# Second biases of a mixture-of-experts block: fp32 products over 8 rows, or fp32r products over 16 rows

## The reference, cut to what matters

```python
combine = jnp.sum(jax.nn.one_hot(idx, E) * w[..., None], axis=-2)          # (tokens, 8)
p1 = jnp.einsum('bsh,eoh->bseo', nf, mlp1_weight) + mlp1_bias
...
act = g * jax.nn.sigmoid(ALPHA * g) * (lin + 1.0)
p2 = jnp.einsum('bsei,ehi->bseh', act, mlp2_weight) + mlp2_bias            # second bias: (8, 256)
combined = jnp.einsum('bseh,bse->bsh', p2, combine)
```

## Time and profile before

| what | value |
|---|---|
| time, median of 3 runs | 1203.12 us (1199.26 to 1204.91) |
| the profiled execution's own time | 1205.98 us |
| its span | 1204.1 us |
| TensorE matmuls busy | 974.9 us (81%) |
| VectorE busy | 828.1 us (69%) |
| ScalarE busy | 697.5 us (58%) |
| GpSimd busy | 424.8 us (35%) |
| mean clock granted to TensorE, share of full | 0.906 |

### The profile page before, as it was taken

The page is one execution under the profiler, slowest core; times in us unless marked ns, Lnnn a source line. Parts: engine busy times, 40 slices in busy tenths (PEclk is TensorE's granted clock), DMA queues, the critical chain, the costliest instruction groups (busy, mean ns, idle before and its releaser), DMA issues.

```text
span 1204.1 us, 18696 instructions
## 1 busy us (share of the span) xinstructions
PE 974.9 (81%) x5241; PEld 414.1 (34%) x5313; DVE 828.1 (69%) x1622; ACT 697.5 (58%) x905; POOL 424.8 (35%) x360
## 2 busy tenths in 40 slices
PE   4608897889679897987778997888799999996564
PEld 1302222233233443333233343323343344344243
DVE  5732102669658797677676799586867897797797
ACT  2318895856448574765448665675567676771232
POOL 2413303433244333533235333542232333233243
PEclk9858998989889999988799898999989899997587
DMA  4254454324424252434413345352534353421011
GB/s 150 74 108 79 102 104 99 88 74 97 116 59 130 77 117 82 102 96 95 119 37 103 98 108 118 71 128 67 114 86 107 97 125 82 101 76 58 31 53 31
DMA packets 80001, 110.08 MB, mean 91 GB/s; under 512 B 22523, under 2 KB 56707, under 8 KB 76803
## 3 DMA queue, kind: packets, MB, share of 16 engines
q1 hardware_dynamic: 61444, 83.47, 29.9%
q10 hardware_dynamic: 18432, 25.17, 7.0%
HBM read 82.89 MB, written 25.69 MB: 90 GB/s over the span
## 4 chain that ended last, share of the span: by engine, by line
PE 49%; DVE 25%; issue 13%; ACT 4%; DMA 3%; POOL 2%; SPq 2%; another core or an unknown queue 1%; DVEq 0%; ACTq 0%; POOLq 0%
PE OP L687 13%; PE S L673 12%; PE D L659 8%; DVE th_sb L1103 3%; DVE act_sb L1108 3%; PE A L642 3%; PE D L569 3%; PE D L586 3%; PE BB L642 3%; DVE acc L1098 2%; DVE g_sb L1086 2%; DVE l_sb L1088 2%; DMA X<-in_x 2%; DVE xn L946 2%; ACT probs L804 2%
## 5 line engine op out<-in xcount | busy, mean ns | idle before, releaser
L804 ACT ACTIVATE probs<-S 128x1024 f32<-128x1024 f32 x512 | 511.8, 1022 | 256.2 <-PE S L673 253.4
L673 PE MATMUL S<-Qs,Ks 98*128 98x512 bf16 x1024 | 312.4, 399 | 61.8 <-issue 23.0
L687 PE MATMUL OP<-probs,V 128*17 128x512 f32 x2048 | 280.1, 620 | 2.7 <-ACT O L813 2.7
L891 POOL TENSOR_TENSOR act_lo<-act_sb,act_hi 128x512 fp32r<-128x512 f32 x128 | 165.5, 1293 | 212.3 <-DVE act_hi L1114 152.4
L673 PEld LDWEIGHTS S<-Qs,Ks 98*128 98x128 bf16 x1024 | 81.4, 101 | 249.0 <-ACT probs L804 98.7
L659 PE MATMUL D<-W,act_hi 128*128 128x256 f32 x448 | 135.6, 333 | 29.5 <-DVE Vn L986 16.2
L1098 DVE SCALAR_TENSOR_TENSOR acc<-D,combh,acc 128x256 f32<-128x256 f32 x224 | 97.1, 475 | 82.5 <-PE D L659 82.1
L1103 DVE SCALAR_TENSOR_TENSOR th_sb<-th_sb,g_sb 128x512 f32<-128x512 f32 x128 | 129.6, 1012 | 0.7 <-ACT th_sb L780 0.7
L885 POOL TENSOR_SCALAR W<-W2b 128x512 fp32r<-128x512 bf16 x64 | 45.4, 709 | 217.4 <-PE D L659 212.1
L1108 DVE SCALAR_TENSOR_TENSOR act_sb<-l_sb,th_sb 128x512 f32<-128x512 f32 x128 | 107.2, 837 | 16.7 <-POOL act_lo L891 12.2
L659 PE MATMUL D<-W,act_lo 128*128 128x256 f32 x448 | 116.3, 290 | 0.0
(11 more groups left out here) (136 smaller groups left out, 1016.7 us busy)
## 6 DMA issues: line engine op xcount, KB each, us to landing
W<-in_w ACTq DMA_DIRECT2D x64, 256.0 KB, 2.7
Ks<-k_scr SPq DMA_DIRECT2D x32, 384.0 KB
W2b<-in_w ACTq DMA_DIRECT2D x64, 128.0 KB, 2.7
Ks<-k_scr SPq DMA_DIRECT2D x32, 256.0 KB
o_scr<-O SPq DMA_DIRECT2D x32, 256.0 KB, 4.5
q_scr<-parts SPq DMA_DIRECT2D x16, 384.0 KB, 3.1
k_scr<-parts SPq DMA_DIRECT2D x16, 384.0 KB, 2.6
Qs<-q_scr SPq DMA_DIRECT2D x32, 192.0 KB
```

The source lines that it names most:

```text
L673: last = mm(S[:, j2, C * i:C * (i + 1)], Ks[0:SROWS + MROWS, g % 2, j, P * kt:P * (kt + 1)], Qs[0:SROWS + MROWS, g % 2, j, :], start=True, ...
L687: last = mm(OP[32 * j:32 * j + VW, :], V[:, kt, HG * g + j, :], probs[:, s % 2, C * j:C * (j + 1)], start=kt == 0, stop=kt == KT - 1)
L804: nc.scalar.activation(probs[:, s % 2, 2 * C * j2:2 * C * (j2 + 1)], S[:, j2, :], ACT.Exp, scale=SCALE).then_inc(exp_done, 1)
L891: tt(act_lo[:, e % 2, it, :], act_sb[:, a % 2, :], act_hi[:, e % 2, it, :].bitcast(FP32), ALU.subtract).then_inc(lo_s, 1)
```

## The change

The combine weights are split into two fp32r parts that together carry the fp32 value, and lie side by side as 16 columns; the bias table is loaded twice, into rows 0 to 7 and 8 to 15, and made fp32r. One product over 16 rows then gives the sum of both parts. The transposes treat the 16 columns as fp32. In `gates2` the sum of the two masks now goes back to `oh1`; a copy rounds it to the first part, `combh` is computed from `oh1`, and a subtraction makes the second part. One more small load is issued near the start.

```diff
-        b2_sb = sb("b2_sb", [NE, E], BF16)
-        b2f = sb("b2f", [NE, E], FP32)
+        b2_sb = sb("b2_sb", [2 * NE, E], BF16)
+        b2f = sb("b2f", [2 * NE, E], FP32R)
...
-        combT = sb("combT", [NE, C], FP32)
+        combT = sb("combT", [2 * NE, C], FP32R)
...
+        comb = sb("comb", [P, TC, 2, NE], FP32R)
...
-        N_LOADS, N_LATE = 6, 11
+        N_LOADS, N_LATE = 6, 12
...
-                (b1_sb[:, :, :, :], b1), (b2_sb[:, :], b2), (rank[:, :], ...
+                (b1_sb[:, :, :, :], b1), (b2_sb[0:NE, :], b2), (b2_sb[NE:2 * NE, :], b2), (rank[:, :], ...
...
-                    pe.wait_ge(comb_s, 3 * (u + 1))
+                    pe.wait_ge(comb_s, 4 * (u + 1))
                     for t in range(TC):
-                        last = nc.tensor.transpose(bank[0:NE, P * t:P * (t + 1)], comb[:, t, :], ident[:, :])
+                        last = nc.tensor.transpose(bank[0:2 * NE, P * t:P * (t + 1)],
+                                                   comb[:, t, :, :].rearrange("p a e -> p (a e)").bitcast(FP32), ident[:, :])
...
-                    v.tensor_copy(combT[:, :], bank[0:NE, :]).then_inc(combT_s, 1)
+                    v.tensor_copy(combT[:, :], bank[0:2 * NE, :]).then_inc(combT_s, 1)
...
-                v.tensor_tensor(comb[:, :, :], oh1[:, :, :], oh2[:, :, :], ALU.add).then_inc(comb_s, 1)
-                dve.wait_ge(comb_s, 3 * u + 1)
-
-                v.tensor_scalar(combh[:, :, :], comb[:, :, :], 0.5, None, ALU.mult).then_inc(comb_s, 2)
+                v.tensor_tensor(oh1[:, :, :], oh1[:, :, :], oh2[:, :, :], ALU.add).then_inc(comb_s, 1)
+                dve.wait_ge(comb_s, 4 * u + 1)
+                v.tensor_copy(comb[:, :, 0, :], oh1[:, :, :]).then_inc(comb_s, 1)
+                v.tensor_scalar(combh[:, :, :], oh1[:, :, :], 0.5, None, ALU.mult).then_inc(comb_s, 1)
+                dve.wait_ge(comb_s, 4 * u + 3)
+                v.tensor_tensor(comb[:, :, 1, :], oh1[:, :, :], comb[:, :, 0, :].bitcast(FP32), ALU.subtract).then_inc(comb_s, 1)
```

More of the change, by code:

```diff
@@ L274, in block_kernel @@
         lgb = sb("lgb", [P, TC, NE], BF16)
-        lgt, pick, oh1, oh2, lg2, comb, combh = (
-            sb(n, [P, TC, NE], FP32) for n in ("lgt", "pick", "oh1", "oh2", "lg2", "comb", "combh"))
+        lgt, pick, oh1, oh2, lg2, combh = (
+            sb(n, [P, TC, NE], FP32) for n in ("lgt", "pick", "oh1", "oh2", "lg2", "combh"))
+        comb = sb("comb", [P, TC, 2, NE], FP32R)
         S = ps("S", [P, 2, 2 * C], FP32)
@@ L403, in _ @@
                 (gate_b_sb[:, :], gate_b[None, :].to_broadcast([P, NE])),
-                (b1_sb[:, :, :, :], b1), (b2_sb[:, :], b2), (rank[:, :], rank_in[None, :].to_broadcast([P, NE])),
+                (b1_sb[:, :, :, :], b1), (b2_sb[0:NE, :], b2), (b2_sb[NE:2 * NE, :], b2), (rank[:, :], rank_in[None, :].to_broadcast([P, NE])),
                 (Ks[SROWS:SROWS + MROWS, :, :, :].rearrange("p s j t -> p (s j t)"), ones_in),
```

## The result

The changed kernel takes 1192.89 us (median of 7 runs, 1189.29 to 1194.83), the kernel before 1203.12 in the same session: a ratio of 0.992, 95% interval 0.9895 to 0.9945, so 0.8% faster and clear of the 0.5% that can be told apart. The profiled execution took 1192.6 us, with a span of 1190.8 and a mean granted clock of 0.918 (0.906 before). The forecast was 1198.0 with a range of 1191 to 1205: the time lies in the range and the direction was right, but the likeliest case, no measurable change, did not come; by the medians the gain is twice the 5.1 us that I summed.

The account below looks back on a forecast made before the run. No single engine was taken to bound the kernel: the chain passes between TensorE (49%) and VectorE (25%). Stages -5.2, additions +1.8 and tail -1.7 us sum to -5.1, from 1203.12 to 1198.0 us, range 1191 to 1205.

Parts of the forecast that it names:

- Where the change lies: Chain holds gates2 and the second b2 stage in chunks 1 to 5, that stage in 6 and 7, both stages in the tail.
- What a stage costs: On TensorE, a b2 stage in fp32r takes 0.43 us at full clock, 0.59 at half; 1.06 and 2.00 before.
- What of it reaches the chain: Second b2 stages of seven chunks: 4.2 to 6.2 us won, 5.2 taken, with ScalarE's exponentials limiting some chunks.
- The additions: Extra VectorE operations in gates2: 0.31 to 0.40 us more in each of the first five chunks, 1.8 us lost in all.
- The tail: Chunk 8, both b2 stages on the chain: 0.9 to 2.45 us won after the added VectorE work, 1.7 taken.
- The sum: Whole kernel: -5.2 + 1.8 - 1.7 = -5.1 us, giving 1198.0 us from the median of 1203.12.
- The clock: Rival: two long slow TensorE stretches of 6.8 us each don't come, 6.8 us more won, 1191 us; chance 0.19.
- The slower rival: TensorE, idler around the second stage, loses its clock more often: even at 1203 us (chance 0.13) or slower, 1209.9 (0.08).
- The gain hidden behind ScalarE: Rival: ScalarE holds TensorE's start behind the stage, so chunks give at most about 2 us, 1202 us; chance 0.08.

Follow-up runs that it names:

- e3: Changed kernel with the first b2 stage of each chunk back in fp32 over 16 rows, only the second in fp32r: 1193.61 us, 0.9934 of the kernel before.
- e4: Changed kernel with the second b2 stage of each chunk back in fp32 over 16 rows, only the first in fp32r: 1200.82 us, 0.999 of the kernel before.
- e5: Changed kernel with fp32r products in the last chunk alone, fp32 over 16 rows in the other seven: 1202.08 us, 0.9972 of the kernel before.
- e9: Changed kernel with the transposes and first b2 stage one half-step earlier (31 and 32), the second left at 34: 1198.4 us, 0.9963 of the kernel before.
- fp32 twin: Kernel before, fp32 over 8 rows without the split, with transposes at 31, first stage at 32, second at 34: 1199.67 us, 0.9972 of the kernel before.
- e7: Changed kernel with all products in fp32 over 16 rows and those of the second b2 stage made twice: 1214.55 us, 1.0089 of the kernel before.
- e1: Changed kernel with all second-bias products back in fp32 over 16 rows, only the additions left: 1202.32 us, 1.0001 of the kernel before.
- e2: Changed kernel with only the rounded first part of the combine weights in 8 rows, no copy, subtraction or second load: 1192.53 us, 0.9913 of the kernel before.
- e10: Changed kernel with four more dependent 128 x 32 VectorE operations in gates2: 1205.08 us, 1.0007 of the kernel before.
- e8: Changed kernel with the second b2 stage one half-step later (35 in place of 34): 1208.24 us, 1.0033 of the kernel before.

## Why the prediction was right and wrong

**Where the change lies: right.** The second stage is on the chain in all seven chunks, the first in the tail alone; e3, e4 and e5 show it, and e9 with its fp32 twin shows that the gain goes when the place is covered.

**What a stage costs: right at full clock.** 0.43 us, as read from the experts' products; 16 rows cost the same as 8 and as 128. At half clock I had 0.59 and the rows show 0.70 to 0.73.

**What of it reaches the chain: a mis-sized term.** I had 4.2 to 6.2 us and took 5.2. The seven stages lost 6.6 us from start to scores. Two things were off. I had capped the chunks 1 and 2 at 0.65 and 0.44 us by ScalarE's exponentials; in the changed kernel's first chunk the scores start at 246.83, while the exponential runs from 246.55 to 247.55, so those scores don't wait for it and the cap was a misreading. And the middle between the two prices was a compromise: the rows of the traces, of e7 too, point to the price at the clock of the place.

**The additions: the other mis-sized term.** I had 0.31 to 0.40 us in five chunks, 1.8 in all, and nothing in 6 and 7. Up to the copy of combT the rows show 0.19 to 0.25 us in every chunk, so the links were cheaper than I had read (0.22, not 0.31, behind a wait). But at the second stage only 0.12 us is left in chunk 1, 0.05 to 0.07 in 2 to 5 and nothing in 6 and 7: 0.4 us. I had taken gates2 as on the chain link by link and not asked what slack lies behind it, between the copy of combT and the copy to acc. Why VectorE is faster there in chunks 1 to 5 is open; the rows show that it is. In chunk 7 the transposes stood 2.1 us, not 3, behind the last of the operations in the kernel before (1034.34 after 1032.27); nothing came of it.

**The tail: a little low.** 1.39 + 1.42 was expected at half clock and (1.98 - 0.70) + (2.01 - 0.73) = 2.6 us measured, 2.3 with the additions, against the 1.7 taken.

**The sum.** 6.6 - 0.4 + 2.3 = 8.5 us, where I had summed 5.1: both main terms erred to the same side. The medians differ by 10.2 us and the ratio says 9.6, with 6.6 to 12.6 as its interval. Taken from the rows directly, as the time from the router's result to the scores behind the second stage, over the seven chunks and the tail, this is what each kernel differs by from the kernel before, beside what its ratio gives:

| kernel | rows, us | ratio, us |
|---|---|---|
| changed | -8.5 | -9.6 |
| e1, all products fp32 | -0.6 | +0.1 |
| e2, one part | -9.4 | -10.5 |
| e3, second stage fast | -7.4 | -7.9 |
| e4, first stage fast | +0.2 | -1.2 |
| e5, tail fast | -2.2 | -3.4 |
| e7, second stage doubled | +10.5 | +10.7 |
| e10, four more operations | -0.5 | +0.8 |

The rows come from one execution of each kernel, all against the same one of the kernel before, and carry about 1 us of chance, the ratios 2 to 3 us; no kernel is off by more than 1.4. So the time of this stretch accounts for the results as well as they are known.

**The clock: the rival that may have taken part.** I gave 0.19 to the clock being lost less often, as a case of its own that ends at 1191, and the measured 1192.89 is nearer to that than to the forecast. I had also named as a sign of being wrong a mean clock that differs from 0.906 by more than 0.005. In the profiled execution it is 0.918, so this sign came. Between the two profiled executions, whose times differ by 13.4 us, the slow stretches differ by 13.7 us, just the two long ones of the rival. Over all runs the mean clock rose less, from 0.910 to 0.915. Over 214 runs of all kernels here, taken within each kernel, a run whose mean clock is 0.001 higher is 0.47 us shorter; 0.005 makes 2.3 us. Added to the 8.5 of the rows, which hold a part of it already, that is 10.8, and with or without it the sum lies in the interval of 6.6 to 12.6. For e10 it makes 9.3 us out of 7.4, where 10.5 was measured. This is a relation between runs, not an experiment: no run here changed the clock and nothing else. But runs of both kernels with the same clock can be compared: at 0.911 and 0.912 the three of the changed kernel have a mean of 1193.7 us and the twelve of the kernel before 1201.8, so 8.1 us of gain are there without any more clock. So the direct part is shown; the clock's share is argued, and why the clock moved is open.

**The slower rival: did not come.** TensorE did become idler in front of the second stage (2.32 us after 1.85), as I had said, and the clock was not lost more often. For this rival I had read that the clock falls behind the long idle times and not behind the short one. Chunk 6 of the kernel before speaks against it: the wait is as short as in chunk 7, and the clock is at half for 6.8 us all the same.

```profile
932.92 1.37 PE L612 MATMUL D<-b2f,combT 8*128 8x256 f32 x4 [0.19 <-DVE acc L1025]
```

Its clock behind the stage, in one of those steps of 1 us:

```profile
935.42:936.42 1.00, 1.00 (x8) 0.00 (x0) 0.93 (x3) 0.90 (x1) 0.00 (x0) 0.50 0.05 4
```

In the changed kernel the wait there is 0.60 us, and the clock stays up. So the length of this wait doesn't tell what the clock does. The Trainium skill's general rule in "TensorE: Matmul & The Clock Gate", "Why this matters for your kernels", to keep TensorE dense, spoke against the change. It is stated for longer gaps than these, so the runs here neither bear it out nor refute it; they show that a wait longer by 0.47 us cost nothing.

**The gain hidden behind ScalarE: wrong.** Had it been so, e3 would have gained little more than its tail.

## What to carry to other kernels

Find the copies of a stage that are on the chain before pricing a faster form of it: of two equal stages here one was worth 0.7% with its tail and the other nothing that could be measured, and both together 0.1% once the table was changed. Price what is removed from the chain at the clock that it ran at, taken from its own rows. Follow what is added up to the point where the chain changes engines, since a short wait on the way can swallow it. And when an engine waits in front of such a stage for a copy that stands behind long work in another engine's queue, give the copy to an engine that idles there; moving the stage in the table only moved the wait.

## What the runs showed that I had not expected

- fp32r products with 16, 8 and 128 rows take the same 0.43 us for two and the step to the next instruction, and a cast from PSUM to fp32r takes VectorE 0.66 us, no less than a copy to fp32.
- One half-step in the table (e8) cost 13 to 15 us, more than the whole change gave.
- Of two small operations of 128 x 32 on VectorE, the one that doesn't wait starts 0.10 us behind the other's start; one that waits for it 0.22 us. The two that the change adds make 0.19 to 0.25 us up to the copy of combT and 0.12 or less at the second stage; four more, 0.85 us or more per chunk, arrive in full and went with 10.5 us of the whole.
